# Last part of a two-layer block: attention one batch after the other, with the first batch's output product and third norm placed in the second's steps

## What is computed

```python
x = x + ga0 * (o * gate) @ Wo.T                 # layer 0, output product
h = layernorm(x) * (1 + cb0) + sb0              # norm 1
x = x + gb0 * (gelu(h @ U1 @ V1 + b1) @ U2 @ V2 + b2)
h = layernorm(x) * (1 + ca1) + sa1              # norm 2
q, k, v = split(h @ w_attn.T)                   # 16 heads of 16
att = softmax(where(mask, q @ k.T / 4, -inf))   # causal, 64 back, 4 global keys
x = x + ga1 * (att @ v) @ w_proj.T
h = layernorm(x) * (1 + cb1) + sb1              # norm 3
h_prev = shift(h, 1)
xr, xk = (m * h + (1 - m) * h_prev for m in (mu_r, mu_k))
x = x + gb1 * sigmoid(xr @ W_r.T) * (relu(xk @ W_k.T) ** 2 @ W_v.T)
```

## Time and profile before

| | |
|---|---|
| median of 3 runs | 2466.02 (2459.04 to 2466.06) |
| the profiled execution | 2457.74, its span 2456.0, mean granted clock 0.945 |
| busy in the span | TensorE 2143.7 (87%), VectorE 1602.1 (65%), ScalarE 1558.3 (63%), GpSimd 1100.0 (45%) |
| chain that ended last | TensorE 44%, VectorE 16%, issue 15%, ScalarE 14%, GpSimd 7% |
| `prob` on GpSimd (L1795) | 256 times, mean 853 ns |
| four transposes of `t` (L1179) | 1024 single ones, mean 282 ns, overlapping |

### The profile page before, as it was taken

The page is one execution under the profiler, slowest core; times in us unless marked ns, Lnnn a source line. Parts: engine busy times, 40 slices in busy tenths (PEclk is TensorE's granted clock), DMA queues, the critical chain, the costliest instruction groups (busy, mean ns, idle before and its releaser), DMA issues.

```text
span 2456.0 us, 88067 instructions
## 1 busy us (share of the span) xinstructions
PE 2143.7 (87%) x32669; PEld 1375.5 (56%) x32669; DVE 1602.1 (65%) x3901; ACT 1558.3 (63%) x4121; POOL 1100.0 (45%) x1221
## 2 busy tenths in 40 slices
PE   7999996878888877885699999999999999999898
PEld 4455452555555555553366565665655756657566
DVE  6888885676776776773277474773746847557465
ACT  6788883676676676664365484564845748547474
POOL 1212223676776777776423344234433343233323
PEclk9999998898998898887799999999999999999999
DMA  6655557333334333411421312312123112220120
GB/s 199 179 154 161 175 152 186 69 67 82 77 68 88 79 69 75 87 32 37 134 69 44 91 22 76 78 45 74 38 76 77 45 52 60 74 72 11 33 52 18
DMA packets 387235, 201.37 MB, mean 82 GB/s; under 512 B 257376, under 2 KB 372704, under 8 KB 386800
## 3 DMA queue, kind: packets, MB, share of 16 engines
q1 hardware_dynamic: 386800, 195.65, 30.3%
HBM read 101.67 MB, written 69.27 MB: 70 GB/s over the span
## 4 chain that ended last, share of the span: by engine, by line
PE 44%; DVE 16%; issue 15%; ACT 14%; POOL 7%; SPq 2%; DMA 1%; ACTq 1%; DVEq 1%; POOLq 0%
PE psum L1050 11%; ACT arena L1569 8%; DVE arena L1861 6%; PE psum L1143 4%; PE psum L1102 3%; PE psum L906 3%; PE psum L1110 3%; PE psum L900 3%; ACT arena L1368 2%; POOL arena L1637 2%; PE psum L1216 2%; PE psum L893 2%; PE psum L914 2%; PE psum L1082 2%; PE psum L1179 2%
## 5 line engine op out<-in xcount | busy, mean ns | idle before, releaser
L1795 POOL TENSOR_TENSOR arena<-arena 128x400 f32<-128x400 f32 x256 | 218.3, 853 | 481.9 <-DVE arena L2223 481.9
L1368 ACT ACTIVATE arena<-psum,scan_sb 64x128 f32<-64x128 f32 x1152 | 307.7, 361 | 115.0 <-PE psum L974 107.0
L1569 ACT ACTIVATE arena<-psum,arena 128x100 f32<-128x100 f32 x1024 | 270.0, 367 | 6.4 <-DVE arena L2215 6.3
L1861 DVE SCALAR_TENSOR_TENSOR arena<-psum,taps_sb,arena 128x511 f32<-128x511 f32 (+2 forms) x288 | 212.5, 747 | 55.1 <-ACT arena L1268 48.4
L808 PE MATMUL psum<-arena,w_in_sb 128*128 128x512 f32 x512 | 230.1, 598 | 1.0 <-ACT arena L1261 1.0
L1611 POOL TENSOR_TENSOR arena<-arena 128x512 f32<-128x512 f32 x64 | 80.7, 1273 | 264.5 <-ACT arena L1294 264.5
L900 PE MATMUL psum<-arena 128*32 128x17 f32 x10240 | 127.3, 192 | 80.7 <-issue 60.0
L1940 DVE TENSOR_TENSOR arena<-psum,scan_sb 64x512 f32<-64x512 f32 x290 | 188.5, 673 | 3.3 <-PE psum L1006 2.9
L2215 DVE TENSOR_REDUCE arena<-psum 128x4 f32<-128x400 f32 x256 | 146.3, 573 | 58.5 <-PE psum L1166 48.1
L1561 ACT ACTIVATE arena<-psum 100x512 f32<-100x512 f32 x256 | 156.1, 610 | 42.8 <-PE psum L1179 36.6
L906 PE MATMUL psum<-arena,scan_sb 128*128 128x512 f32 (+1 forms) x328 | 172.3, 612 | 11.1 <-ACT psum L1413 4.5
(11 more groups left out here) (225 smaller groups left out, 4711.7 us busy)
## 6 DMA issues: line engine op xcount, KB each, us to landing
...
arena<-k_rows_d SPq DMA_DIRECT2D x128, 68.0 KB, 2.1
arena<-v_rows_d SPq DMA_DIRECT2D x128, 68.0 KB, 2.3
...
```

Of the source, the lines that this page charges most:

```text
L1368: ins = act.activation(dst.rearrange("p (t x a) -> p t x a", x=PP, a=INNER)[upper, :, x], src.rearrange("p (t a) -> p t a", a=INNER)[upper ...
L1569: act.activation(c_soft[s][:, f % 2, u], sc, ACT.Exp, bias=c_max[s][:, u:u + 1]).then_inc(c_act.mark(f"exp{s}{f}u{u}"), 1)
L1795: pool.tensor_tensor(soft, soft, c_rec[s].unsqueeze(2).broadcast_to([P, 4, KEYS]), ALU.mult).then_inc(c_pool.mark(f"prob{s}{f}"), 1)
L1861: ins = dve.scalar_tensor_tensor(out=a_acc[:, t, j:TOK], in0=bank[2 + t][:, 0:TOK - j], scalar=taps_sb[:, t % KT, col:col + 1], in1=a_acc[ ...
```

## The change

`ATT` runs all 16 frames of slot 0 and then those of slot 1; soft tiles, banks and scalars alternate by step as before (`t % 2`), score banks are 0/1 and 3/4, the value products alternate between banks 5 and 6 by quarter, and bank 7 (`SPARE`) is free for other work. In front of it slot 0 is turned and projected (`turn2`, `vt`, `q`, `k`) and then slot 1, each in one go. In slot 1's steps stand, for slot 0: `wp` (TensorE steps 14 and 22), its add and statistics (VectorE 15, 16, 23, 24), the spread's root (ScalarE 25), normalisation (VectorE 26, 27), `turn3` (28, 30) and `h3` (29, 31), and `d0`, `xr0`, `xk0` (VectorE 32 to 34); the next pair's statistics stand in VectorE's steps 5, 6, 9 and 10 and its root in ScalarE's step 12; `wp10` in step 32 and `r0` in step 35. Step 15 is the last of slot 0, so `wp` and the later work of slot 0 can only follow the quarters named in the waits. Behind the attention come `kk0`, `wp11`, next transposes, `vv0`, next `u1` of slot 0, and then slot 1's norm 3 and channel mix. The next pair's `u1` and its eviction `p` move from the head of the loop to its end. Slot 1's shift difference is VectorE's, not GpSimd's. The root is made with Ln and Exp (one table set with the softmax's Exp), VectorE's reciprocals of it go, and of the fillers only those of the last pair's norm 2 stay. SyncE's program is not touched. The channel mix's tiles of a slot lie over that slot's own queries and keys.

The core of the diff (`rows_half`, `turn_half`, `projected`, `receptance`, `hidden`, `mixed`, `values`, `queries`, `keys` are the old bodies cut into functions):

```diff
-c_qb = [carve(KT, FRAMES, 4 * QF) for _ in SLOTS]
-keys_at = top[0]
-c_k = [carve(KT, FRAMES, KEYS) for _ in SLOTS]
+c_qb, c_k, region = [], [], []
+for _ in SLOTS:
+    region.append(top[0])
+    c_qb.append(carve(KT, FRAMES, 4 * QF))
+    c_k.append(carve(KT, FRAMES, KEYS))
 values_at = top[0]
 c_v = [carve(FRAMES, DIM) for _ in SLOTS]
...
-ATT = [(f, s) for f in range(FRAMES) for s in SLOTS]
+ATT = [(f, s) for s in SLOTS for f in range(FRAMES)]
+QUARTERS = len(ATT) // QTR
 T_LAG, PV_LAG, YE_LAG, Y_LAG = 3, 4, 5, 6
-WARM = {"s0": 9, "t0": 6, "t1": 4, "pv0": 4, "t2": 2, "pv1": 2, "norm1": 10, "u10": 6, "u11": 6, "norm2": 22, "vt0": 8, "vt1": 6, "norm3": 10, "turn30": 6, "turn31": 8, "pv28": 1, "t29": 1, "pv29": 1, "t30": 2, "pv30": 2, "t31": 2, "pv31": 2}
-TURNED, Y_BANKS = 2, (3, 6, 7)
...
+PE_SIDE = {14: ["wp00"], 22: ["wp01"], 28: ["turn300"], 30: ["turn301"],
+           32: ["wp10"], 35: ["r00", "r01"]}
+ACT_SIDE = {25: ["ln30", "rstd30"], 29: ["h300"], 31: ["h301"]}
+DVE_SIDE = {15: ["x300"], 16: tile_names("st3", 0, (0, 1)),
+            23: ["x301"], 24: tile_names("st3", 0, (2, 3)) + tile_names("ag3", 0, range(TT)), 26: tile_names("xh3", 0, (0, 1)),
+            27: tile_names("xh3", 0, (2, 3)), 32: ["d0"], 33: ["xr00", "xr01", "x310"], 34: ["xk00", "xk01"] + tile_names("st3", 1, (0, 1))}
...
+    + ["turn200", "turn201", "vt00", "vt01", "q00", "q01", "k00", "k01", "turn210", "turn211", "vt10", "vt11", "q10", "q11", "k10", "k11"] + att_pe()
+    + ["kk00", "kk01", "wp11", "vv00", "vv01", "turn310", "turn311", "r10", "r11", "kk10", "kk11", "vv10", "vv11"])
 c_pool = Steps(sem("c_pool"),
...
+def next_u1(n, s):
+    pe.wait_ge(n_act.sem, n_act.at(n, f"h{s}1"))
+    for k in range(KT):
+        mm = pe.matmul(bank[(2, 4)[s]][half(s)], u1_sb[:, k], c_h[s][:, k, 1:TOK + 1], start=(k == 0), stop=(k == KT - 1))
+    mm.then_inc(n_pe.mark(f"u1{s}"), 1)
...
+    turn_2(0, (1, 2))
+    pe.wait_ge(c_act.sem, c_act.at(i, "h201"))
+    values(0, (1, 2))
+    if ahead:
+        pe.wait_ge(n_dve.sem, n_dve.at(i + 1, "x01"))
+    columns(0, "q", (3, 0))
+    if ahead:
+        pe.wait_ge(n_dve.sem, n_dve.at(i + 1, "x11"))
+    columns(0, "k", (7, 4))
+    turn_2(1, (5, 6))
+    pe.wait_ge(c_act.sem, c_act.at(i, "h211"))
+    pe.wait_ge(c_dve.sem, c_dve.at(i, "vt01"))
+    values(1, (1, 2))
+    columns(1, "q", (5, 6))
+    pe.wait_ge(c_dve.sem, c_dve.at(i, "ks03"))
+    pe.wait_ge(c_act.sem, c_act.at(i, "ks03"))
+    columns(1, "k", (7, 4))
...
+            at = SCORES[t % 2]
+            if t >= 2:
+                pe.wait_ge(c_act.sem, c_act.at(i, step_name("exp", t - 2) + f"u{QUADS - 1}"))
...
+        if t == 14:
+            pe.wait_ge(c_dve.sem, c_dve.at(i, "y01"))
+            pe.wait_ge(c_pool.sem, c_pool.at(i, "wp0"))
+            projected(0, 0, bank[SPARE])
+        if t == 22:
+            pe.wait_ge(c_dve.sem, c_dve.at(i, "y03"))
+            projected(0, 1, bank[SPARE])
+        if t == 28:
+            pe.wait_ge(c_dve.sem, c_dve.at(i, "xh303"))
+            turn_half(0, 0, c_pe, "turn3", bank[SPARE])
+        if t == 30:
+            pe.wait_ge(c_act.sem, c_act.at(i, "h300"))
+            turn_half(0, 1, c_pe, "turn3", bank[SPARE])
+        if t == 32:
+            pe.wait_ge(c_act.sem, c_act.at(i, "h301"))
+            pe.wait_ge(c_dve.sem, c_dve.at(i, "y11"))
+            pe.wait_ge(c_pool.sem, c_pool.at(i, "wp1"))
+            projected(1, 0, bank[SPARE])
+        if t == 35:
+            receptance(0, (3, 4))
...
+    hidden(0, (0, 1))
+    pe.wait_ge(c_dve.sem, c_dve.at(i, "y13"))
+    projected(1, 1, bank[5])
+    if ahead:
+        next_turn(i + 1, 0)
+    pe.wait_ge(c_act.sem, c_act.at(i, "kk01"))
+    mixed(0, (0, 1))
+    if ahead:
+        next_u1(i + 1, 0)
+    pe.wait_ge(c_dve.sem, c_dve.at(i, "xh313"))
+    turn_half(1, 0, c_pe, "turn3", bank[7])
+    turn_half(1, 1, c_pe, "turn3", bank[5])
+    receptance(1, (5, 6))
+    if ahead:
+        pe.wait_ge(n_act.sem, n_act.at(i + 1, "p0"))
+    hidden(1, (7, 2))
+    if ahead:
+        pe.wait_ge(c_act.sem, c_act.at(i, "r01"))
+        next_turn(i + 1, 1)
+        pe.wait_ge(n_act.sem, n_act.at(i + 1, "h10"))
+    pe.wait_ge(c_act.sem, c_act.at(i, "kk11"))
+    mixed(1, (3, 7))
+    if ahead:
+        next_u1(i + 1, 1)
...
+        act.activation(c_std[s], c_mv[s][:, :, 1], ACT.Ln, bias=parity[:, 6:7]).then_inc(c_act.mark(f"ln{stage}{s}"), 1)
+        act.wait_ge(c_act.sem, c_act.at(i, f"ln{stage}{s}"))
+        act.activation(c_rstd[s], c_std[s], ACT.Exp, scale=-0.5).then_inc(c_act.mark(f"rstd{stage}{s}"), 1)
...
+    act.preload_act_table_set("natural_log_exp_and_others")
+    std(2, 0)
+    modulate(2, 0, 0, bank[1])
+    modulate(2, 0, 1, bank[2])
+    std(2, 1)
+    values(0, bank[1])
+    queries(0, bank[3])
+    modulate(2, 1, 0, bank[5])
+    modulate(2, 1, 1, bank[6])
+    keys(0, bank[4])
+    values(1, bank[1])
+    queries(1, bank[5])
+    keys(1, bank[4])
...
+        if t == 12 and ahead:
+            next_std(i + 1)
+        if t == 25:
+            std(3, 0)
+        if t == 29:
+            modulate(3, 0, 0, bank[SPARE])
+        if t == 31:
+            modulate(3, 0, 1, bank[SPARE])
...
+    hidden(0, (0, 1))
     if ahead:
-        for s in SLOTS:
-            act.wait_ge(c_dve.sem, c_dve.at(i, f"xk{s}{KT - 1}"))
-            if s == 1:
-                act.wait_ge(c_pool.sem, c_pool.at(i, "d1"))
-            next_modulate(i + 1, s)
+        next_modulate(i + 1, 0)
+    std(3, 1)
+    if ahead:
+        next_p(i + 1, 0)
+    modulate(3, 1, 0, bank[7])
+    modulate(3, 1, 1, bank[5])
+    receptance(0, (3, 4))
+    receptance(1, (5, 6))
+    hidden(1, (7, 2))
+    if ahead:
+        act.wait_ge(c_dve.sem, c_dve.at(i, "xk11"))
+        next_modulate(i + 1, 1)
+        next_p(i + 1, 1)
...
-    pool.wait_ge(c_act.sem, c_act.at(i, f"h31{KT - 1}"))
-    pool.tensor_tensor(c_d[1], c_h[1][:, :, 1:TOK + 1], c_h[1][:, :, 0:TOK], ALU.subtract).then_inc(c_pool.mark("d1"), 1)
...
+    residual_2(0)
+    statistics(2, 0, range(TT))
+    spread(2, 0)
+    residual_2(1)
+    normalise(2, 0, range(TT))
+    statistics(2, 1, range(TT))
+    spread(2, 1)
+    if ahead:
+        next_sum(i + 1, 0)
+    normalise(2, 1, range(TT))
+    if ahead:
+        next_sum(i + 1, 1)
+    values(0, bank[2])
+    queries(0, bank[0])
+    keys(0, bank[7])
+    values(1, bank[2])
+    queries(1, bank[6])
+    keys(1, bank[7])
...
+        if t in (5, 9) and ahead:
+            next_stats(i + 1, t // 9, (0, 1))
+        if t in (6, 10) and ahead:
+            next_stats(i + 1, t // 10, (2, 3))
+            next_spread(i + 1, t // 10)
+        if t == 15:
+            residual(3, 0, 0, "wp", bank[SPARE])
+        if t == 16:
+            statistics(3, 0, (0, 1))
+        if t == 23:
+            residual(3, 0, 1, "wp", bank[SPARE])
+        if t == 24:
+            statistics(3, 0, (2, 3))
+            spread(3, 0)
+        if t == 26:
+            normalise(3, 0, (0, 1))
+        if t == 27:
+            normalise(3, 0, (2, 3))
+        if t == 32:
+            shift(0)
+        if t == 33:
+            mix(0, 0, "xr", c_xr[0])
+            residual(3, 1, 0, "wp", bank[SPARE])
+        if t == 34:
+            mix(0, 1, "xk", c_xk[0])
+            statistics(3, 1, (0, 1))
...
+        dve.wait_ge(c_pe.sem, c_pe.at(i, "turn301"))
+        next_normal(i + 1, 0)
+    residual(3, 1, 1, "wp", bank[5])
+    statistics(3, 1, (2, 3))
+    spread(3, 1)
+    normalise(3, 1, range(TT))
+    shift(1)
+    mix(1, 0, "xr", c_xr[1])
+    mix(1, 1, "xk", c_xk[1])
+    if ahead:
+        dve.wait_ge(c_pe.sem, c_pe.at(i, "turn311"))
+        next_normal(i + 1, 1)
+    for s, banks in enumerate(((0, 1), (3, 7))):
         for a in range(2):
+            dve.wait_ge(c_act.sem, c_act.at(i, f"r{s}{a}"))
             dve.wait_ge(c_pe.sem, c_pe.at(i, f"vv{s}{a}"))
...
```

More of the change, by code:

```diff
@@ L1103, in up @@
                         mm.then_inc(c_pe.mark(f"v1{s}{f}"), 1)
+                pe.wait_ge(c_dve.sem, c_dve.before(i, "rv01"))
                 for f in range(UP_BANKS):
@@ new lines, in columns, with projected @@
+                def columns(s, which, banks):
+                    for m in range(KT):
+                        j = ("q", "k").index(which) * KT + m
+                        for k in range(KT):
+                            mm = pe.matmul(bank[banks[m]][:], w_attn_sb[:, k, j * P:(j + 1) * P], c_h[s][:, k, 1:TOK + 1],
+                                           start=(k == 0), stop=(k == KT - 1))
+                        mm.then_inc(c_pe.mark(f"{which}{s}{m}"), 1)
+                def projected(s, a, dst):
+                    rows_half(s, a, c_pe, "wp", lambda k, t: c_y[s][:, t, k], lambda k: c_wp[s][:, k], dst)
@@ L1524, in pair, with hidden @@
+                def hidden(s, banks):
+                    for m in range(KT):
+                        act.wait_ge(c_pe.sem, c_pe.at(i, f"kk{s}{m}"))
```

(15 more changed lines are left out.)

546 lines of the change are left out of this document (239 added, 307 removed).

## The result

The change makes the kernel slower: 2548.41 us (median of 4, 2540.98 to 2555.07) against 2463.53 (median of 4), a ratio of 1.0346 with a 95% interval of 1.0304 to 1.0387. The profiled execution took 2554.34 around a span of 2552.5, at a mean granted clock of 0.922, where before it was 0.945. The forecast was 2480: right in its sign, 68 us short in size, and outside its range.

A forecast was written before the change was run, and what follows sets the result against it. TensorE was taken to bound the attention steps (1.58 each). Parts summed to 155.8 a pair, 159.0 with clock falls (+1.9); seven pairs 13.3 plus the last 1.3 gave 2472 profiled, 2480 as median, range 2438 to 2508.

The forecast's parts named there:

- the feed-forward's -0.7: First v1 to norm 2's transposes: u1 and its copy leave the loop's head, u2 follows v1 after 1.9, not 2.6.
- two falls, 3.2: TensorE's clock falls twice a pair, once for the 4.3 wait, once for the group before: 2 x 1.6 = 3.2.
- Norm 2 to the first scores, 25.1: Norm 2's transposes to first scores: waits 1.35 and 1.2 plus 22.5 of products, 25.1 instead of 28.5.
- (a) to (d): Attention, first scores to step 32: quicker ramp, moved products 4.4, stalls 7.3, evictions -0.6; given as +9.5, 52.7 to 62.2.
- Term (b): Attention steps: two output-product halves at 1.72 and two transpose groups at 0.47, moved in and paid in full: 4.4.
- (c): Stalls at attention steps 5 to 30 from side work on VectorE and ScalarE, 7.3 together; step 28 1.4, step 30 1.6.
- From Z on: Start of step 32 to the next v1: 47.8 to 41.1, -6.7, with 4.3 of idle before r1.
- B: Rival: side work fits at steps 5 to 30, half of 7.3 stall goes, -1.8 a pair net, about 2452; chance 0.20.
- C: Rival: the clock falls only at the 4.3 wait, +0.3 a pair, 2468, no change; chance 0.20.
- D: Rival: half of the 7.3 attention stalls and no clock fall at all, -5.0 a pair, 2425; chance 0.12.
- E: Rival: clock falls at two more waits, the ramp and step 14, +3.2 a pair, 2506; chance 0.12.
- F: Rival: an unseen wait on each of two removed table loads, 20 less in all, 2460, inside no change; chance 0.03.

The follow-up runs named there:

- e1: The kernel after, with the second slot's next u1 product moved ahead of that slot's last value product: 2547.0 us.
- e5: e4 with GpSimd's gates of wp and wv and its pads held until VectorE has normalised both slots for norm 2: 2468.6 us.
- e3: The kernel after, with idle products in TensorE's waits at steps 0 to 2, 28, 30, 32 and ahead of r1: 2498.6 us.
- e4: e3 with both slots' next u1 side by side in one bank, the first slot's copy of p moved accordingly: 2485.6 us.
- e6: e5 with the next pair's statistics moved out of the attention steps to VectorE's gaps between the projections: 2458.2 us.
- e8: e6 with norm 3's second turn in another bank, first turn and h300 one step later, four idle products left of steps 28 to 32: 2422.6 us.

## Why the prediction was right in its sign and wrong in its size

I had 159.0 a pair; the mean of seven is 168.2, so 9.2 are missing. Two steps of the forecast failed most: the feed-forward's -0.7, which left out ScalarE's loop turn, and the clock's "two falls, 3.2". By stretch:

- **Feed-forward, "-0.7", the step that failed first.** I had the Gelu table's load begin with the last copy of `p`, at no cost. ScalarE's loop turn stands between them, and before the change the first `u1` products and their copies covered TensorE's side of it. The wait that lies open costs 2.9 in the six pairs behind a turn and 0.9 in the first, +2.6 in the mean. In three pairs the clock also fell as `u2` began behind it, for 1.3 to 2.9: +0.8 in the mean. So the part took 30.8 and not 27.4. e1 shows that `u2` can come 2.0 behind `v1`, e5 that the time is then won, falls included: 52.7 from `v1` to the scores, where I had 27.4 + 25.1 = 52.5.
- **Norm 2 to the first scores, 25.1:** right (25.3 in all seven pairs, at clock 1.00), waits of 1.10 and 1.18 included: +0.2.
- **Attention.** Without the clock e3 has 61.8 to the last scores, where I had 62.2 - 1.6 = 60.6: +1.2. (My terms (a) to (d) add up to 9.3, and I wrote 9.5.) Term (b) and the steady 1.58 hold. Of (c), step 28 was 2.37 and not 1.4; the others came close (0.9, 1.36, 2.17 against 1.1, 1.6, 2.05). The row that I had not costed is this one of VectorE, and GpSimd's beside it:

```profile
1655.32 1.27 DVE L2285 TENSOR_SCALAR arena<-arena 128x256 f32<-128x256 f32 x2
```

```profile
1655.47 0.97 POOL L1914 TENSOR_TENSOR arena<-arena 128x400 f32<-128x400 f32 x1 [0.83 <-DVE arena L2370]
```

  Two tiles take 1.27 and the next two 1.24, where four take 1.38 elsewhere: +1.1. The held one ends at 1656.59, 0.15 behind GpSimd's product (1656.44). That this delay is the same as the one of e1 is argued from the rows; no run took it away in the steps.
- **From Z on.** I charged the moved `u1` nothing beside its old place, but apart they take 1.93 each and together 1.95. e3's tail is 44.3, my 41.1 + 1.6 = 42.7: +1.6. e4, with the two together, has 43.0, so 1.3 of it is theirs. The wait at `r1` (4.3 forecast, 3.8 found) and at `vv1` (1.0) were right.
- **The clock, "two falls, 3.2".** e3 measures 5.9 in attention and tail: +2.7. I took the fillers' removal at the ramp for a gain and put the first fall behind the longer waits; the ramp, with waits of 1.06, 0.36 and 0.48 around short products, fell in the pair shown to 0.51 over 5.9 us, and step 7 began 12.7 behind step 0. In four pairs of seven it did not fall, and the 10.5 that I had was right (10.3).

2.6 + 0.8 + 0.2 + 1.2 + 1.6 + 2.7 = 9.1 of the 9.2. The last pair cost 5.0 and not 1.3. The profiled execution also entered the last part 12.5 later, of which some 11 had passed before its first product, in code that the change leaves alone; over the fourteen traces here the first `v1` lies between 1202 and 1223, so that is no effect of the change, and the medians' gap of 85 is the better figure.

That the sign was right was partly luck. By the forecast the kernel would have been faster but for the clock (155.8 a pair). e3, with the clock at 1.00 in attention and tail, still takes 162.4, against 156.9 before.

**The rivals.** B (side work fits) is out: the waits are all there, and e6 gains 10 us by taking some of it away. C and D (one fall or none) are out by the clock's rows. E (falls at two more waits, 2506) was nearest; the ramp fell as it said in three pairs of seven, step 14 in none. The Trainium skill's remark on transposes, cited there, can't be judged by these runs, since the ramp's scores are short products as well. F is out: e3 to e5 explain the time without any unseen cost of a table load. Six falls, the most that I had thought possible (9.6 a pair), would have covered the clock's part; at 2531 they lay outside my range, and even they leave out the three plain terms of 2.6, 1.6 and 1.2, which I had at nothing. And the order itself isn't slow: with e8's edits it takes 151.4 a pair against 156.9.
